# Experts: second half of the transposed output turned behind six products, and a subtraction moved from GpSimd to VectorE

## The reference, cut to what matters

```python
capacity = max(1, int(Sz * CAP_FACTOR / E) + 1)          # 257
gate_vals, sel_idx = jax.lax.top_k(scores_t, capacity)
tokens = x[b_idx, sel_idx]
h = jnp.einsum('becd,edh->bech', tokens, w1) + b1[None, :, None, :]
h = jax.nn.gelu(h, approximate=False)
y = jnp.einsum('bech,ehd->becd', h, w2) + b2[None, :, None, :]
gated = y * gate_vals[..., None]
out = jnp.zeros_like(x).at[b_idx, sel_idx].add(gated)
```

## Time and profile before

| | |
|---|---|
| median of 3 runs | 836.5 us (834.14 to 836.87) |
| profiled execution, whole | 829.58 us |
| its span, first to last instruction | 827.6 us |
| PE busy | 759.7 us (92%) |
| PE weight loads | 620.7 us (75%) |
| DVE busy | 535.4 us (65%) |
| ACT busy | 388.9 us (47%) |
| POOL busy | 321.2 us (39%) |
| the eight experts | about 611 us to the end of the span |

### The profile page before, as it was taken

How to read it: one execution, slowest core, us unless ns; L and a number is a source line. 1 busy time by engine, 2 the same in 40 slices (tenths; PEclk the granted TensorE clock), 3 DMA queues, 4 the chain that set the end, 5 groups by cost and what they waited for, 6 DMA issues and landing times.

```text
span 827.6 us, 12893 instructions
## 1 busy us (share of the span) xinstructions
PE 759.7 (92%) x4925; PEld 620.7 (75%) x4925; DVE 535.4 (65%) x1148; ACT 388.9 (47%) x678; POOL 321.2 (39%) x279
## 2 busy tenths in 40 slices
PE   7899988999999999999999979985589999999995
PEld 7765555755666555588979878884479999999995
DVE  7777784576576585266454589884747756667552
ACT  3555544454455435465372345343025755557550
POOL 5511002100111023047371043343426778887794
PEclk9999999999999999999999999996799999999998
DMA  7000000000000100010011200212202354444522
GB/s 185 1 1 0 1 0 1 1 1 1 0 1 1 51 3 1 0 52 3 1 38 62 93 10 18 86 52 64 102 27 83 106 145 147 122 121 112 138 33 32
DMA packets 21509, 39.31 MB, mean 47 GB/s; under 512 B 4913, under 2 KB 16905, under 8 KB 19145
## 3 DMA queue, kind: packets, MB, share of 16 engines
q1 hardware_dynamic: 14793, 30.07, 11.0%
q0 software_dynamic: 6656, 8.43, 5.8%
HBM read 29.96 MB, written 8.40 MB: 46 GB/s over the span
## 4 chain that ended last, share of the span: by engine, by line
PE 59%; DVE 16%; ACT 4%; issue 3%; POOL 3%; ACTq 0%; DVEq 0%
PE ps L477 18%; PE ps L639 9%; PE ps L1165 6%; PE ps L1168 5%; PE ps L743 5%; PE ps L660 2%; PE ps L661 2%; PE ps L601 2%; DVE rep L1761 1%; DVE sm L1562 1%; PE ps L1089 1%; DVE Pb L1566 1%; PE ps L471 1%; DVE sm L1571 1%; POOL out_dram L2653 1%
## 5 line engine op out<-in xcount | busy, mean ns | idle before, releaser
L639 PE MATMUL ps<-PT,VA 128*65 128x512 f32 (+1 forms) x288 | 147.5, 594 | 1.6 <-ACT PT L2059 1.3
L2059 ACT ACTIVATE PT<-ps 128x512 f32<-128x512 f32 x128 | 75.7, 592 | 63.5 <-PE ps L661 63.4
L477 PE MATMUL ps<-GT,wh 128*128 128x258 f32 (+1 forms) x768 | 94.7, 284 | 1.3 <-DVE GT L1859 1.3
L477 PEld LDWEIGHTS ps<-GT,wh 128*128 128x128 f32 x768 | 92.7, 189 | 1.6 <-DVE GT L1859 1.6
L2653 POOL DMA_INDIRECT out_dram<-ye,idx x40 | 69.7, 1742 | 19.7 <-issue 10.9
L2410 POOL TENSOR_TENSOR ssq<-ssq,half 128x8 f32<-128x8 f32 x16 | 26.1, 1639 | 122.5 <-DVE ssq L1287 122.5
L2350 ACT ACTIVATE het<-ps,b1e 128x514 f32<-128x514 f32 x64 | 44.3, 692 | 58.4 <-PE ps L477 54.0
L1894 DVE TENSOR_TENSOR he<-het,he 128x514 fp32r<-128x514 f32 x64 | 46.4, 726 | 35.7 <-ACT he L1923 35.1
L660 PE MATMUL ps<-QA,KA 128*128 128x512 f32 x144 | 68.5, 476 | 0.4 <-ACT QB L1923 0.4
L2400 POOL TENSOR_TENSOR rs<-rs,half 128x4 f32<-128x4 f32 (+2 forms) x19 | 18.2, 956 | 122.9 <-DVE rs L1206 95.0
L601 PE MATMUL ps<-KA,QA 128*128 128x368 f32 x192 | 59.7, 418 | 3.9 <-DVE x L1371 2.9
(11 more groups left out here) (289 smaller groups left out, 1643.7 us busy)
## 6 DMA issues: line engine op xcount, KB each, us to landing
wr<-in_w1e_dram SPq DMA_DIRECT2D x8, 1024.0 KB, 4.8
wr<-in_w2e_dram SPq DMA_DIRECT2D x8, 1024.0 KB, 4.8
x<-in_x_dram SPq DMA_DIRECT2D x4, 512.0 KB, 6.4
w<-in_w_dram SPq DMA_DIRECT2D x2, 1024.0 KB, 5.4
y_dram<-yr SPq DMA_DIRECT2D x3, 512.0 KB, 3.0
out_dram<-x SPq DMA_DIRECT2D x3, 512.0 KB, 4.0
b2r<-in_b2r_dram SPq DMA_DIRECT2D x8, 128.0 KB, 3.2
gt<-y_dram,idx POOLq DMA_INDIRECT x40, 3.0
```

The lines of the kernel that those rows point to most:

```text
L477: op = pe.matmul(o, l, r, start=n == 0, stop=n == len(calls) - 1)
L639: pe.matmul(bank[6 + hf][0:65, :], VA[b][0:K, kt, h, :], PT[u % 4][0:K, :], start=kt == 0, stop=kt == 8).then_inc(p_pv, 1)
L2059: a.activation(PT[u % 4][0:K, :], bank[4 + u % 2][0:K, :], ACT.Exp, bias=0.0 if K == 128 else mcol[:, b:b + 1]).then_inc(a_exp, 1)
```

## The change

Two edits in the expert loop.

On TensorE the six transposes of `yT`'s rows stand after the sixth product of round 2 instead of after the twelfth. The wait for `a_yT` moves with them.

On POOL the two subtractions of 512 elements become one, elements 0 to 511 of the next second weights' low part. Elements 512 to 1023 go to DVE: a `tensor_tensor` in round 3, after the second of that round's side steps and ahead of row block 0, with a wait for ACT's fourth copy of the expert (`a_wh`). POOL's counter `g_wh` goes up by two per expert instead of three, and the waits of PE and SP on it follow. DVE's counter `v_wh` is unchanged: its next increment, by L1911, comes after the new instruction.

```diff
@@ tensor_program
-                        if n_ == 2 and n == 11:
+                        if n_ == 2 and n == 5:
                             pe.wait_ge(a_yT, 2 * ex + 2)
                             rows_out(ex, 0, ((6, (2, 3)), (7, (4,))))
...
-                    pe.wait_ge(g_wh, 2 + 3 * (ex - 1) + 1)
+                    pe.wait_ge(g_wh, 2 + 2 * (ex - 1) + 1)
...
-                    pe.wait_ge(g_wh, 2 + 3 * ex)
+                    pe.wait_ge(g_wh, 2 + 2 * ex)
@@ vector_program
                     if n_ == 2:
                         rows_out(ex, ((6, (2, 3)), (7, (4,))))
+                    if n_ == 3 and ex + 1 < NE:
+                        w2n, c = wh2[(ex + 1) % 2], slice(512, 1024)
+                        v.wait_ge(a_wh, 2 + 6 * ex + 4)
+                        v.tensor_tensor(w2n[1][:, c], wr[1][:, c], f(w2n[0][:, c]), ALU.subtract)
                     next(side_, None)
                     next(side_, None)
                 row_out(ex, 0)
@@ gpsimd_program
                 gated_row(ex)
                 if ex + 1 < NE:
-                    w2n = wh2[(ex + 1) % 2]
-                    for i in range(2):
-                        c = slice(512 * i, 512 * i + 512)
-                        g_.wait_ge(a_wh, 2 + 6 * ex + 2 + i + 1)
-                        g_.tensor_tensor(w2n[1][:, c], wr[1][:, c], f(w2n[0][:, c]), ALU.subtract).then_inc(g_wh, 1)
+                    w2n, c = wh2[(ex + 1) % 2], slice(0, 512)
+                    g_.wait_ge(a_wh, 2 + 6 * ex + 3)
+                    g_.tensor_tensor(w2n[1][:, c], wr[1][:, c], f(w2n[0][:, c]), ALU.subtract).then_inc(g_wh, 1)
@@ sync_program
-                    sp.wait_ge(g_wh, 2 + 3 * ex + 1)
+                    sp.wait_ge(g_wh, 2 + 2 * ex + 1)
...
-                    sp.wait_ge(g_wh, 2 + 3 * ex + 3)
+                    sp.wait_ge(g_wh, 2 + 2 * ex + 2)
```

## The result

The changed kernel takes 860.1 us (median of 6, 855.97 to 864.5), the kernel before, run beside it, 836.6 us: ratio 1.0297, interval 1.027 to 1.0323. It is slower by 3%, outside the forecast range of 833.0 to 838.8.

The account below looks back on a forecast made before the run. PE was taken to set the pace in the experts, with stops and five scatters in the last. From profiled 829.58 us, +1.1 - 0.55 - 0.67 = -0.1 gave 829.5, carried over to 836.4 us; range 833.0 to 838.8.

Parts of the forecast that it names:

- part 2: Moving 512 elements from POOL to DVE: free in experts 0 to 5, -0.67 us through expert 6's earlier scatters.
- Price 0: DVE's extra 0.60 us per expert, and POOL's earlier finish in experts 0 to 5, were each claimed to cost nothing.
- the fit by 0.1 us: DVE's last row block, pushed back 0.60 us, ends at 747.37, before the next expert's first he at 747.47.
- Part 1: Transposes six products earlier: +1.1 us over experts 0 to 6 from PE's wait for yT, -0.55 us in the last.
- My 0.04 for the restart: Extra PE time after each wait for yT, added to 0.12 us to make 0.16 us per expert.
- Rival A: Slower: PE's wait for a_yT costs 0.5 us per expert or more; 839.9 us at 0.6; chance 0.07.
- Expert 6: DVE's 512 elements were taken to go before POOL's remaining subtraction, bringing the first scatter 0.67 us sooner.
- the -0.67: Gain at PE's restart in the last expert from earlier scatters and gb2; bounds 0 and -0.85 us.
- rival D: The POOL and DVE edit does nothing and the last expert's PE stop stays: +0.55, 837.1 us; chance 0.3.
- Rival B: Faster: POOL is the hidden bound and gets 1.2 us per expert off, 8.5 us in all, 828; chance 0.02.
- Rival C: Slower: DVE's spare 0.1 us is gone, he comes late in every expert: +3.5, 840.0 us; chance 0.02.
- The 7 us: Timed median 836.5 us lies 7 us above the profiled run; place unknown in the trace, difference carried over.

Follow-up runs that it names:

- e10: Kernel before plus a one-input VectorE reduction of 512 elements where the change puts its subtraction: 859.59 us, ratio 1.0328.
- e9: Changed kernel with GpSimd's gathers held until VectorE's 1024-element subtraction is done: 835.55 us, ratio 1.0025.
- e5: Kernel before with the 512 elements moved to VectorE inside its existing subtraction, one of 1536 behind row block 0; transposes unmoved: 836.3 us, ratio 1.0021.
- e15: Changed kernel with the gathers also waiting for VectorE's scaling of row block 0: 842.35 us, ratio 1.0073.
- e7: Kernel before with the fetch of raw second weights held until row block 1 is scaled: 834.56 us, ratio 0.9995.
- e8: Changed kernel with the fetch of raw second weights held until the next expert's fourth he: 858.26 us, ratio 1.0296.
- e6: Kernel before plus an extra 512-element VectorE subtraction into scratch behind the 1024-element one: 837.85 us, ratio 1.0032.
- e13: Changed kernel with the first three scatters of experts 0 to 6 cut to 2 rows each: 863.94 us, ratio 1.0319.
- e11: Changed kernel with the first three scatters held until VectorE has made the next expert's sixth he: 843.08 us, ratio 1.013.
- e4: Kernel before, GpSimd keeping both subtractions, plus a 512-element VectorE subtraction into scratch at the change's place: 850.52 us, ratio 1.0183.
- e12: Changed kernel with every gather from the third expert on cut to 2 rows: 838.94 us, ratio 1.0056.
- e1: Kernel before with only the transposes moved, from behind twelve to behind six products: 835.61 us, ratio 0.9999.
- e2: Kernel before with only the 512-element subtraction moved from GpSimd to VectorE; transposes stay behind twelve products: 855.65 us, ratio 1.0244.
- e3: Kernel before with GpSimd spared one subtraction, which VectorE makes in expert 0 only and which is otherwise left out: 835.35 us, ratio 1.002.
- e14: Changed kernel with both gathers and the first three scatters cut to 2 rows: 844.18 us, ratio 1.0108.

## Why the prediction was wrong, step by step

**The step that failed** is in part 2, on VectorE: "Price 0", and with it, on GpSimd, "the gathers start where they did. Price 0". Both statements were right about what they named. The gathers do start where they did (0.37 us ahead of the first gelu in both kernels), and `he` is on time: row block 1, behind L1915, ends at 739.07 and the first `he` starts at 739.16, so the fit by 0.1 us held. What I didn't ask was what the gathers' *length* hung on. Their 1.62 us lay right behind the start of L1911, 0.48 us apart, and I had used that very blocking twice, for expert 6 and the last expert, but only where it made somebody late. Here it made GpSimd late in a way that helped. With it gone the fifth gather ends at 5.72 us behind the first gelu instead of 6.97. Its price is 4.75 us of lateness per expert, all eight blocks together, six times: 28.5 us of the 29.3 found above, where the sum had nothing. On TensorE it is 18.3 us more idle time ahead of the first products, and 10.0 us more in them.

**What is shown and what isn't.** Shown: the loss comes with a first gather that gets in ahead of the 1024-element subtraction, in every kernel of the table; it comes without any two-input instruction added (e10), and goes with the gathers held until the subtraction is over (e9) or another place for the same work (e5), and for the most part with the first gather held by one row block (e15). Shown too: neither the weight fetch (e7, e8), nor 0.6 us more of VectorE's work by itself (e6), nor the scatters' data (e13) bring it. The size isn't settled by the first gather: with the same one of 1.02 us, e11 and e4 lose 9 and 15 us, e10 26. Not shown: why TensorE's count goes up 1 to 4 us late while GpSimd issues its DMAs at an even pace of 1.25 us. The ends of products are modelled in the profile, so it can't be told whether the products or only their count were late. The fetching of instructions, which the trace records as DMA packets, is not the reason as far as they show: one falls into 1 of the 18 late stretches of after. Nor is the pace the whole rule: e15, e6 and before have their fifth gather end at the same 6.97 and are late by 1.51, 0.75 and 0 us per expert. Whether the gathers' data have a share wasn't told apart (e12).

**Part 1** was right in kind and small in size. ScalarE writes the second half of `yT` from 729.26 to 729.74, and the weight loads of the transposes start at 729.79. That is 0.84 us after the first of the six loads ahead of them (728.95), where six unbroken ones take 0.72: a wait of 0.12 us, as worked out. The chain of after:

```profile
729.23 0.71 PE ps L1168 x6
729.94 0.73 PE ps L1101 x6
730.67 2.13 PE ps L1168 x18
```

Transposes and 24 products take 3.57 us, in before 1.43 + 0.66 + 1.42 = 3.51 us, so +0.06 us per expert where I had 0.16. My 0.04 for the restart was not there. It came from a misread row besides: the 3.49 us of 27 products behind 810.20 are 0.27 us more than 27 at the pace of the 12 in 1.43, not within 0.1; after has 3.51 at that place. And the range, as added up, would begin at 832.5, not 833.0. Neither changes the outcome. At the end six products stand ahead of the transposes instead of twelve. From the last expert's first gelu to the first of the five last scatters before has 19.47 us, e7 (the same order of work there) 18.58, and e1 17.95: against e7 that is -0.63 where I had -0.55, against before it would be -1.5. With part 2 in both, after against e2 gives -0.65 (18.26, 18.91). Rival A (0.5 us per expert and more) didn't happen. In after the end looks like this, five scatters after one another as in rows 3:

```profile
841.05 3.51 PE ps L1165 x27
844.56 0.71 PE ps L1168 x6
845.27 0.53 PE ps L1101 x4
...
845.92 0.49 DVE ye L1871
846.41 0.27 issue
846.68 1.58 POOL out_dram L2657
```

**Expert 6** went the other way than I let it go. VectorE and GpSimd in after:

```profile
823.11 3.36 DVE L1907 TENSOR_TENSOR wh<-wr,wh 128x512 fp32r<-128x512 f32 x1
...
823.05 1.63 POOL L2665 TENSOR_TENSOR gb<-b2r,gate 128x512 f32<-128x512 f32 x1
824.05 1.87 POOL L2681 TENSOR_TENSOR wh<-wr,wh 128x512 fp32r<-128x512 f32 x1
```

"I let DVE go first" was wrong: VectorE was held over both of GpSimd's, to 825.92, and ended 0.55 behind. GpSimd kept its turn, which was my case with bounds 0 and -0.8. Whether the -0.67 came depends on the kernel to compare with. By the stretch from the last gelus to the scatters, e2, part 2 alone, has 18.91 us: 0.56 less than before's 19.47, but 0.33 more than e7 and e4 (18.58), which have GpSimd's part as in before. TensorE's stop of 0.64 us is the difference. It is there in before and again in e6 and e10 (0.65, 0.64 us; 19.52, 19.48), and not in e1, e4 or e7. In before the first scatter in expert 7's time starts 0.18 us behind the first `he` subtraction and takes 1.97 us; in e7 it is recorded 0.02 us behind it and takes 1.58. So the end of before hangs on the order of two instructions as well, and what part 2 is worth there, and with it rival D, stays open. In after VectorE's `he` is still held (2.17 us from 835.57, TensorE's loads idle 0.26 us instead of 0.85).

**Rival B** (GpSimd is the hidden bound) is refuted by e3: it is spared 1.2 us per expert and the time is that of before. **Rival C** had the right engine, the right place and the right sign, at a chance of 0.02 and a price of 3.5 us. Its mechanism, a late `he`, isn't what happened.

**The 7 us** between the profiled execution of before (829.58) and its median, which I carried over without a place: they go with the granted clock. Of the executions of before timed beside e12 to e14, those at a mean granted clock of 0.981 to 0.983 took 831.9 to 833.1 us, those at 0.969 took 839.6 to 840.6. In the first 100 us the clock is 1.00 in before's profile, 0.97 in e1's and e7's and 0.98 in e9's, and these three reach the first gelu of expert 1 at 649.07, 647.15 and 645.79 us instead of 642.83. They are also late at block 7 in each expert, by 0.35 to 0.52 us, where before is not. Carrying the difference over was sound.

## What the runs showed of the hardware

A gather of GpSimd that starts behind a VectorE subtraction with two inputs in SBUF is held for the rest of it. A 128-row gather then ended 0.88 to 0.90 us behind the end of the `wh` subtraction, however long that was (a gather of 1.62 us in before, 2.15 in e5, 1.23 in e15 where it came late), and in e6, where a second subtraction follows at once, behind that one's (2.22 us). When the gather was recorded 0.11 us or more ahead, it took 1.02 us; recorded 0.01 us ahead, it was the one held. So the recorded start is about 0.1 us off the moment that decides. The other way round nothing is held: the 1024-element subtraction took 1.20 us in every kernel that has it, beside a gather that was first too (after, e2, e4, e8, e10, e11, e13), whereas beside GpSimd's subtractions it took 3.06.

The Trainium skill, page "SBUF — State Buffer", section "Who interferes with whom", says that such an instruction and a GpSimd instruction that reads SBUF lock each other out and that issue order decides. The gathers here agree that order decides, but they are locked out and do not lock out: 1.62 us against 1.20 unchanged. The same section reports that a `tensor_tensor` did not stall a DMA of GpSimd's, and infers that the descriptors need only the write interface, which a `tensor_tensor` leaves free. Here a `tensor_tensor` holds back the issue of a gather: 1.62 to 2.22 us for a gather that takes 1.02 when it is first.

The second thing was unexpected altogether: five gathers in a row at 1.25 us and a scatter behind them, issued beside TensorE's dense products, came with a count of finished blocks that TensorE raised up to 4.05 us after the last product's record, and with gelus 1.1 and 2.8 us late on average. With the first gather held up by 0.6 us none was late at blocks 4 and 5. The third is the clock: in four of the six experts of after it fell beside the stop, and 24 products took 4.53 instead of 3.25 us at a granted clock of 0.64. The length of the stop alone doesn't tell: the clock stayed at 1.00 behind one of 2.62 us (expert 4), and was 0.57 over the 3.56 us behind one of 1.87 in e8.

## What to carry to other kernels

Where an engine has slack, its work is free but its order is not: before an instruction is put ahead of another, ask which instruction of another engine overlaps that other one now, and whether its length contains a wait that somebody profits from. An instruction form with two different lengths (here, for the same 128 rows, a gather of 1.62 us and one of 1.04) is the sign of such a hidden coupling. And where a small edit costs nearly six times its own work (23.5 us for seven times 0.6), change its place and its cover before its amount: one placement (e5) or one wait (e9) told more than any further sum, and both bring the moved work back to the time of before, though none of these kernels beat it.
